# Preparation of a bidirectional layer by halves of the batch and on 128 rows, with gate projections of 32 rows each

## The reference, cut to what matters

```
xn     = layernorm over channels of X
for direction in (forward, backward, on the flipped sequence):
    z, xbc, dt = split(xn @ in_proj)                 # z: 64 gates, xbc: 64 x + 16 B + 16 C, dt: 4 heads
    x, B, C    = split(silu(depthwise_conv4(xbc)))   # causal, 4 taps
    dt         = softplus(dt + dt_bias);  a = -exp(A_log) * dt
    y          = sum over earlier tokens of (C.B) * exp(sum of a between them) * x * dt,  + D * x
    out       += rmsnorm(y * silu(z)) @ out_proj
X = X + average of both directions
```

## Time and profile before

| | |
|---|---|
| median of 3 runs (lowest, highest) | 698.82 us (697.15, 700.01) |
| the profiled execution: its time, span from first to last instruction | 702.39 us, 700.5 us |
| busy: PE, DVE, ACT, share of the span | 71%, 44%, 46% |
| mean granted TensorE clock | 0.740 of 2.4 GHz |

### The profile page before, as it was taken

The page is one execution under the profiler, slowest core; times in us unless marked ns, Lnnn a source line. Parts: engine busy times, 40 slices in busy tenths (PEclk is TensorE's granted clock), DMA queues, the critical chain, the costliest instruction groups (busy, mean ns, idle before and its releaser), DMA issues.

```text
span 700.5 us, 10770 instructions
## 1 busy us (share of the span) xinstructions
PE 495.4 (71%) x3956; PEld 274.8 (39%) x3957; DVE 308.5 (44%) x724; ACT 320.1 (46%) x1085; POOL 0.2 (0%) x4
## 2 busy tenths in 40 slices
PE   5654555556987689999855666666576898989633
PEld 2221222223663567677513333333322454455211
DVE  1174000006883678888751000000018896477443
ACT  2232333333672767777633333333335655655411
POOL 0000000000000000000000000000000000000000
PEclk9555555556899899999985555555568999999877
DMA  4000000000000000000000000000024110000000
GB/s 190 0 2 1 0 1 1 0 1 0 2 1 1 0 2 1 1 2 1 1 0 1 0 1 1 0 1 0 1 43 98 39 36 1 1 2 3 0 9 32
DMA packets 9389, 8.37 MB, mean 12 GB/s; under 512 B 3314, under 2 KB 9074, under 8 KB 9204
## 3 DMA queue, kind: packets, MB, share of 16 engines
q1 hardware_dynamic: 9332, 7.62, 3.8%
HBM read 4.99 MB, written 0.52 MB: 8 GB/s over the span
## 4 chain that ended last, share of the span: by engine, by line
PE 58%; DVE 16%; ACT 15%; issue 7%; SPq 1%; DMA 1%; DVEq 1%; ACTq 0%
PE ps L317 16%; ACT arena L335 10%; PE ps L295 4%; PE ps L300 3%; PE ps L620 2%; PE ps L637 2%; PE ps L817 2%; PE ps L781 2%; PE ps L624 2%; DVE arena L1316 2%; PE ps L651 2%; DVE arena L1325 2%; PE ps L796 2%; PE ps L257 2%; PE ps L785 2%
## 5 line engine op out<-in xcount | busy, mean ns | idle before, releaser
L317 PE MATMUL ps<-arena,wsb 16*16 16x16 f32 (+1 forms) x1024 | 131.5, 206 | 116.9 <-ACT arena L335 111.4
L335 ACT ACTIVATE arena<-ps 16x16 f32<-16x16 f32 (+1 forms) x512 | 96.0, 188 | 192.4 <-PE ps L317 192.4
L317 PEld LDWEIGHTS ps<-arena,wsb 16*16 16x16 f32 (+1 forms) x1024 | 76.7, 118 | 200.3 <-ACT arena L335 186.9
L341 DVE TENSOR_TENSOR X<-X,ps 128x128 f32<-128x128 f32 x16 | 4.6, 287 | 199.6 <-PE ps L300 199.5
L1033 ACT ACTIVATE arena<-ps,arena 128x128 f32<-128x128 f32 (+1 forms) x128 | 52.3, 418 | 31.1 <-DVE arena L1317 31.0
L1121 ACT ACTIVATE arena<-ps 128x512 f32<-128x512 f32 x72 | 40.9, 595 | 25.9 <-PE ps L785 20.4
L1467 DVE TENSOR_TENSOR arena<-arena,ps 128x512 f32<-128x512 f32 x64 | 41.8, 682 | 16.0 <-ACT arena L1121 13.6
L1316 DVE TENSOR_REDUCE arena<-ps 128x2 f32<-128x512 f32 (+1 forms) x48 | 33.0, 688 | 18.3 <-PE ps L620 10.9
L637 PE MATMUL ps<-wsb,arena 128*128 128x128 f32 x192 | 30.7, 283 | 11.3 <-DVE arena L1325 11.2
L624 PE MATMUL ps<-arena 128*128 128x256 f32 x128 | 35.4, 400 | 0.0
L1325 DVE TENSOR_TENSOR arena<-arena 128x512 f32<-128x512 f32 x48 | 33.3, 693 | 1.7
(11 more groups left out here) (267 smaller groups left out, 764.5 us busy)
## 6 DMA issues: line engine op xcount, KB each, us to landing
wsb<-weights SPq DMA_DIRECT2D x1, 2060.5 KB, 9.2
arena<-xn SPq DMA_DIRECT2D x16, 128.0 KB, 2.5
arena<-w SPq DMA_DIRECT2D x20, 64.0 KB
wsb<-weights SPq DMA_DIRECT2D x1, 549.5 KB, 4.3
X<-x SPq DMA_DIRECT2D x1, 512.0 KB, 3.4
out<-arena SPq DMA_DIRECT2D x2, 256.0 KB, 2.3
arena<-w_biases SPq DMA_DIRECT2D x20, 17.0 KB
csb<-consts SPq DMA_DIRECT2D x1, 128.0 KB, 9.1
```

The costliest lines, as they stand in the source:

```text
L317: nc.tensor.matmul(step_columns(k, rows, r), w_state, states[0:rows, :, :, t].rearrange("p g j -> p (g j)"), start=False, stop=True, skip_ ...
L335: nc.scalar.activation(states[0:rows, :, :, t + 1].rearrange("p g j -> p (g j)"), step_columns(t // STEP_BANK, rows, t % STEP_BANK), func) ...
```

## The change

The stack is made in two sets of 16 DMAs, first columns of j = 0, 1 for all taps and groups, as soon as half 0 of `xn` is there, then j = 2, 3. The first direction's x, B and C are projected and passed through silu half by half, in banks given by `FIRST_X` and `FIRST_BC`. dt lies on 128 rows by 512 columns (half h in rows 64h to 64h + 63) in place of 64 by 1024; scans are four, the three bf16 parts are made for both directions at once on 128 rows in `sum_parts`, and `place_sums` copies the rows of one direction into `c3`, six copies. Two of the eight operands of the first direction are made in slot 1 of its loop. The first direction's exponents use bank (n + 2) % 4, its first C.B products come after exponent 1, and only exponent 2 waits for `xdt`. `project_z` issues eight matmuls of 32 rows by 64 columns per direction, one for each batch group and half, each reading only its group's partitions. The diff at its core:

```diff
+FIRST_X, FIRST_BC = ((5, 6), (0, 1)), ((7, 2), (4, 3))
+TURNED = ((5, 6, 0, 1), (0, 1, 2, 3))
...
-        def decay_part(link, d, part):
-
-            rows, dst = cs[ROWS * d:ROWS * (d + 1)], c3[ROWS * part:ROWS * (part + 1)]
-            link(nc.vector.tensor_copy(dst, rows))
-            if part < 2:
-                link(nc.vector.tensor_tensor(rows, rows, dst, ALU.subtract))
+        def place_sums(d):
+
+            for part in range(3):
+                for h in range(2):
+                    ins = nc.vector.tensor_copy(c3[ROWS * part:ROWS * (part + 1), 2 * h:2 * h + 2],
+                                                sum_parts[E2 * h + ROWS * d:E2 * h + ROWS * (d + 1), part])
+            return ins
...
-            sp.wait_ge(s["normalised"], 8)
-            for i in range(K):
-                for g in range(G):
-                    sp.dma_start(xs[C * i:C * i + C, :, g, K - 1 - i:K - 1 - i + T],
-                                 xn[C * g:C * g + C, :].rearrange("p (j t) -> p j t", j=J)).then_inc(s["M stack"], 16)
+            sp.wait_ge(s["normalised"], 7)
+            for h in range(2):
+                if h == 1:
+                    sp.wait_ge(s["normalised"], 8)
+                for i in range(K):
+                    for g in range(G):
+                        sp.dma_start(xs[C * i:C * i + C, 2 * h:2 * h + 2, g, K - 1 - i:K - 1 - i + T],
+                                     xnj[C * g:C * g + C, 2 * h:2 * h + 2, :]).then_inc(s[("M stack", "M stack rest")[h]], 16)
...
-                mm = nc.tensor.matmul(ps[0:2 * ROWS, 4 + h, :], W("M_dtW"), halves(xn)[h], start=True, stop=True)
+                pe.wait_ge(s["normalised"], 7 + h)
+                mm = nc.tensor.matmul(ps[E2 * h:E2 * (h + 1), 4, :], W("M_dtW"), halves(xn)[h], start=True, stop=True)
...
-                for gp in range(2):
-                    for h in range(2):
-                        nc.tensor.matmul(ps[:, 2 * gp + h, :], W(("fwd", "bwd")[d] + "_z")[:, gp * P:(gp + 1) * P], halves(xn)[h],
-                                         start=True, stop=True).then_inc(s["M z proj"], 1)
+                for h in range(2):
+                    for g in range(G):
+                        rows, gp, gl = slice(C * g, C * (g + 1)), g // 2, g % 2
+                        mm = nc.tensor.matmul(ps[E2 * gl:E2 * (gl + 1), 2 * gp + h, :],
+                                              W(("fwd", "bwd")[d] + "_z")[rows, gp * P + gl * E2:gp * P + (gl + 1) * E2],
+                                              halves(xn)[h][rows, :], start=True, stop=True)
+                        if gl == 1:
+                            mm.then_inc(s["M z proj"], 1)
...
             project_z(0)
             pe.wait_ge(s["M weights"], 1)
             pe.wait_ge(s["M stack"], 16 * K * G)
+            project_x_first(0)
+            pe.wait_ge(s["M dt"], 1)
...
+            mm.then_inc(s["M dt turned"], 1)
+            project_bc_first(0, 0)
+            pe.wait_ge(s["M stack rest"], 16 * K * G)
             pe.wait_ge(s["M z"], 4)
-            project_x(0)
...
+            project_x_first(1)
+            pe.wait_ge(s["M dt by token"], 1)
+            project_bc_first(1, 0)
+            project_bc_first(0, 1)
+            project_bc_first(1, 1)
...
+                    if d == 0 and n == 2:
+                        pe.wait_ge(s["M xdt"], 1)
+                    if d == 0 and n == 5:
+                        pe.wait_ge(s["M decay operands"], 2)
...
-                    gp, h = k // 2, k % 2
+                    gp, h = k % 2, k // 2
                     act.wait_ge(s["M z proj"], 4 * d + k + 1)
...
             for part in range(3):
-                decay_part(link, 0, part)
-            for k in range(G + HEADS):
+                link(nc.vector.tensor_copy(sum_parts[:, part], cs))
+                if part < 2:
+                    link(nc.vector.tensor_tensor(cs, cs, sum_parts[:, part], ALU.subtract))
+            link(place_sums(0))
+            for k in (0, 1, 4, 5, 6, 7):
                 ins = decay_operand(0, k)
...
                         if d == 0:
+                            for k in (2, 3):
+                                ins = decay_operand(0, k)
+                            ins.then_inc(s["M decay operands"], 1)
...
-                    if d == 0 and n in (8, 10, 12):
-                        decay_part(link, 1, n // 2 - 4)
+                    if d == 0 and n == 8:
+                        dve.wait_ge(s["M decay operands"], 2)
+                        link(place_sums(1))
```

More of the change, by code:

```diff
@@ L746, in _ @@
                 for i in range(2):
[L747 to L750, removed]
+                    if d == 0:
+                        continue
+                    pe.wait_ge(s["M mean squares saved"] if i == 0 else s["M out saved"], 2 if i == 0 else 1)
                     for h in range(2):
@@ L758, in _ @@
                     project_z(1)
-                pe.wait_ge(s["M decay operands"], d + 1)
-                pe.wait_ge(s["M xdt"], d + 1)
-                pe.wait_ge(s["M C"], d + 1)
+                pe.wait_ge(s["M decay operands"], 1 if d == 0 else 3)
+                if d == 1:
+                    pe.wait_ge(s["M xdt"], 2)
+                pe.wait_ge(s["M C"], d + 2)
                 pe.wait_ge(s["M z"], 4 * (d + 1))
@@ L784, in exponent, with cb_products @@
                     c0 = j * T + block_of(d, which) * P
-                    nc.tensor.matmul(ps[:, n % 4, :], key_side[d][g // 2][:, g % 2, c0:c0 + P],
+                    nc.tensor.matmul(ps[:, ring(n), :], key_side[d][g // 2][:, g % 2, c0:c0 + P],
                                      query_side[d][:, :, c0:c0 + P], start=False, stop=True).then_inc(s["M exponent"], 1)
[L787 to L799, removed]
+                def cb_products(k):
+                    if k < 8:
+                        pe.wait_ge(s["M B split"], G * d + (2 if k == 0 else 4))
+                    if k >= 8:
+                        pe.wait_ge(s["M gram"], ALL * d + slot_of(k - 5) + 1)
+                    for i in range(4):
+                        one, piece = near_unit(k + i)
+                        at0 = block_of(d, piece) * P
+                        mm = nc.tensor.matmul(ps[:, 4 + k // 4 % 2, i * P:(i + 1) * P],
+                                              bz[:, one % G, one // G, at0:at0 + P],
+                                              cpj[:, one // G, at0:at0 + P], start=(i == 0), stop=(i == 3))
+                    mm.then_inc(s["M CB"], 1)
                 def near_products(k):
@@ L1088, in squares, with silu_x_first @@
                 nc.scalar.activation(zf[:, j, :], yg[:, j, :], ACT.Square).then_inc(s["M squares"], 1)
+            def silu_x_first(h):
+                for gp in range(2):
+                    act.wait_ge(s["M x proj"], 2 * h + gp + 1)
+                    nc.scalar.activation(xf[:, 2 * h:2 * h + 2, gp * T:(gp + 1) * T],
+                                         ps[:, FIRST_X[h][gp], :].rearrange("p (j t) -> p j t", j=2), ACT.Silu, bias=W("fwd_bx"))\
+                        .then_inc(s["M x"], 1)
@@ L1090, in _, with silu_bc_first @@
+            def silu_bc_first(i, h, n):
+                act.wait_ge(s["M bc"], n)
+                nc.scalar.activation(halves((bp, cp)[i])[h], ps[:, FIRST_BC[i][h], :], ACT.Silu, bias=W(("fwd_bB", "fwd_bC")[i]))\
+                    .then_inc(s[("M B", "M C")[i]], 1)
             gates(0)
             for d in range(2):
-                name = ("fwd", "bwd")[d]
-                if d == 1:
-                    act.wait_ge(s["M y"], J)
[L1096 to L1099, removed]
-                                         ps[:, k, :].rearrange("p (j t) -> p j t", j=2), ACT.Silu, bias=W(name + "_bx"))\
-                        .then_inc(s["M x"], 1)
@@ L1102, in _ @@
-                if d == 0:
-                    act.wait_ge(s["M dt turned"], 1)
-                    nc.scalar.activation(dtt.rearrange("p a b -> p (a b)"), ps[:, 6, :], ACT.Copy).then_inc(s["M dt by token"], 1)
-                if d == 1:
+                if d == 0:
+                    silu_x_first(0)
+                    act.wait_ge(s["M dt turned"], 1)
+                    nc.scalar.activation(dtt.rearrange("p c h r -> p (c h r)"), ps[:, 4, :], ACT.Copy).then_inc(s["M dt by token"], 1)
+                    silu_bc_first(0, 0, 1)
+                    silu_x_first(1)
+                    silu_bc_first(1, 0, 2)
+                    silu_bc_first(0, 1, 3)
+                    silu_bc_first(1, 1, 4)
+                else:
+                    act.wait_ge(s["M y"], J)
+                    for k in range(4):
+                        gp, h = k // 2, k % 2
+                        act.wait_ge(s["M x proj"], 4 * d + k + 1)
+                        nc.scalar.activation(xf[:, 2 * h:2 * h + 2, gp * T:(gp + 1) * T],
+                                             ps[:, k, :].rearrange("p (j t) -> p j t", j=2), ACT.Silu, bias=W("bwd_bx"))\
+                            .then_inc(s["M x"], 1)
@@ L1396, in _ @@
```

(1 more changed line is left out.)

102 lines of the change are left out of this document (53 added, 49 removed).

## The result

The kernel after the change takes 705.79 us, the median of 4 runs (702.8 to 707.86); the kernel before, run beside it on the same chip, 697.99 us (4 runs). The ratio is 1.0107, 95% interval 1.0056 to 1.0159. The change costs about 1.1%, some 7.5 us. The profiled execution took 706.23 us, with a span of 704.4 us and a mean granted clock of 0.739 (before: 702.39, 700.5, 0.740).

The account below looks back on a forecast made before the run. The prediction took stack transfers, then PE and DVE, to bound the first direction's preparation, and PE its loop. First product +4.9, operands +0.8, loop end -0.5 and gates -0.9 gave +4.3 on 698.82, so 703.1 us, range 695 to 706.5.

Parts of the forecast that it names:

- The issue time goes with the form: Stack DMAs on SP's queue: halving the bytes leaves the time from issue to issue at 0.63 us; chance 0.60.
- follows the bytes: Rival for the stack issues: spacing falls to 0.34 us with the bytes, giving 692.5 us; chance 0.15.
- the two-row stores: Rival for the stack issues: each takes 0.49 us, as two-row stores to memory did, giving 698.0 us; chance 0.17.
- T2: First direction's preparation: moment the stack's second half is usable, forecast at 540.9 us, 8.0 us after the stack before.
- The chain behind T2: First direction: work left from T2 to the loop's first product, 10.5 us at full clock.
- The clock, "I take 1.6 (0 to 2.4)": Work behind T2: PE's lower clock level after idling some 4 us adds 1.6 us, range 0 to 2.4.
- Two operands in slot 1: First direction's loop: two operands moved into slot 1 stand between products on DVE, counted as +0.8 us.
- The loop's pace: Loop slots 9 to 32: PE sets the pace, so they stay unchanged at 24.6 us.
- The end of the loop: First direction, slot 32 to last product: six small copies replace `decay_part`, -0.5 us (0 to -0.6).
- Gates: Second direction's gate projections: 32-row matmuls run together in fours and ACT sets the end, -0.9 us (0 to -1.0).
- Serial gate matmuls: Rival for the gate projections: matmuls run one after another, 6.9 us in place of 3.7, giving 707.2 us; chance 0.05.
- The preparation on 128 rows is covered: First direction's dt and operands on DVE: the saving on 128 rows is hidden by the late stack, DVE needed only about 547.

Follow-up runs that it names:

- e3: Kernel before, each of the 16 stack DMAs moving one 1 KB row in place of four (output not the reference's): 697.1 us, single run.
- e2: Kernel before with the stack made by 32 DMAs in two halves, PE waiting for all of them at once: 706.29 us, ratio 1.0115.
- e6: Changed kernel plus six useless matmuls keeping PE busy ahead of its wait for the stack's second half: 701.94 us, ratio 1.0068 to the kernel before.
- e5: Kernel before with only the gate projections changed, to eight matmuls of 32 rows per direction, and the gates in that order: 696.14 us, ratio 0.997.
- e1: Changed kernel with the stack made again by 16 DMAs of both halves: 697.12 us, ratio 0.9986 to the kernel before.
- e4: Changed kernel with the last 12 of the 32 stack DMAs issued by ACT, the others by SP: 698.05 us, ratio 1.0001 to the kernel before.
- e8: Changed kernel, each half's stack 10 issues on SP and 6 on ACT, x turned by halves before B and C, eight operands before the loop: 692.45 us.
- e7: Changed kernel with 16 stack DMAs, x turned before the last three quarters of B and C, all eight operands before the loop: 698.59 us, ratio 0.9995.

## Why the prediction came out as it did

It forecast 703.1 us and slower; it is 705.79 and slower, inside the range and 2.7 above the forecast, but above the 701 to 705.5 that the forecast's own terms gave. As a difference, +4.3 us was forecast and some +7.5 measured. The first product, forecast at 552 to 554, came at 555.7 on the count of the kernel before (518.14 + 37.57). The mechanism held, and one term was too small.

- **The issue time goes with the form: right.** 32 issues, 0.66 us apart (21.15 / 32), for half the bytes; e3 shows it for a quarter. The rivals "follows the bytes" (0.34) and "the two-row stores" (0.49) fall with it. By the Trainium skill (Perfetto Trace Analysis, DMA Optimizations) splitting may let some transfers start sooner where the DMA engines are generally idle; here the queue, not the engines, was full, and e2 shows that the split alone costs 1.15%.
- **T2, 540.9 forecast: nearly right.** Counted from `xn` it was forecast 22.76 us behind (540.9 - 518.14) and came 23.42 behind: 0.66 more. The last issue started 20.55 us after the first, not 19.5, half of it because one of them took 1.11 us; the way from it to the work was 2.1 us, not 2.5.
- **The chain behind T2, at full clock 10.5 us: right.** e6 took 10.73.
- **The clock, "I take 1.6 (0 to 2.4)": this is the term that was mis-sized.** The kernel after takes 14.15 us behind T2, so it was 3.65, beyond its upper end too; PE had waited 5.79 us, not some 4. x took 3.61 from T2 to B and C where 1.7 were counted, B and C 3.75 where 2.7, the C.B products with their handover 1.91 where 1.2, and the turning, `times_dt` and `split_b` what was forecast. I took two thirds of the 2.4 us that one x projection had lost. Here all of the second half's x and the start of B and C had the lower level, and a second stretch followed at the C.B products, which the forecast did not know. With e6's extra matmuls both are gone. Had this term been 3.65, the forecast would have been 705.2 us. First product: 0.66 + 2.05 of clock make 2.7 on top of +4.9, and it was +7.58.
- **Two operands in slot 1, +0.8: right**, +0.93 (9.21 us from the first product to slot 9 against 8.28). **The loop's pace: right**, 24.59 us from slot 9 to 32. **The end of the loop, -0.5: right**; slot 32 to the last product took 6.29 against 6.71, so -0.4. **Gates, -0.9: right**, -1.14, here and in e5.
- **Serial gate matmuls: wrong**, as expected. 16 matmuls of 0.43 us would take 6.9 and took 1.95. The Trainium skill (TensorEngine Tiling (Array Packing), Restrictions and Gotchas) has different row tiles unable to access one PSUM bank at the same time; on separate partitions of a bank this case does not bear that out.
- **The preparation on 128 rows is covered: right**, DVE idles 15.31 us behind it.

With the measured terms the sum is 7.58 + 0.93 - 0.42 - 1.14 = +6.95 us; the timed ratio gives 7.5, with an interval of 3.9 to 11.1. That the table has +6.88 at the next norm is in part luck: 1.6 us that the forecast did not know were gained ahead of the second direction, 1.3 of them by the clock, and 1.6 were lost again behind it (+5.32 there, +6.88 at the norm). e1 and e2 close the account from both sides: without the split no loss, with the split alone all of it.

## What to carry to other kernels

Before a transfer is split so that work may start on its first part, ask what paces the issues: look at the engine's queue beside the DMA share, and if the issues follow each other without a gap, expect a split to lengthen them: here 16 issues of 10.52 us became 32 of 21.15, with the DMA engines at 0.44. Try a second queue for the issues first. And price PE's waits twice: once for the wait and once for the work behind it, which may run at half the clock. That can happen at a later and shorter wait of the chain too; here the same wait of 2.05 us had it in one kernel and not in three others.

## What the runs showed of the hardware

- A DMA of 32 partitions within SBUF takes the issuing queue 0.63 to 0.69 us from one to the next (16 in 10.15 and 10.52 us, 32 in 20.65 to 21.97), with 128, 64 or 32 KB in it. ACT's queue has the same pace (12 in 7.89 us, 11 in 7.10), and both run at it side by side. The Trainium skill (DMA: Bandwidth & Descriptors, Issuing engines are not separate DMA queues) says that starting DMAs on several engines saves only the sequencer's time, which is usually small next to the DMA; here an issue is 0.60 of the 0.66 us from one DMA to the next, and e4 (ratio to the kernel before 1.0001, with one queue 1.0107) and e8 gained from it.
- The granted clock fell to 1.2 GHz behind waits of PE of 5.79 and, in the kernel after, of 2.05 us, and cost 3.4 us in a chain of 14. In e6 the same wait of 2.05 us, with PE kept busy in the earlier one, left the clock at 2.4 GHz, as it did in e1 and e4. A wait of 1.44 us left it there in e1 (x projection 3.65 us) and not in e7 (5.35 us).
- Sixteen matmuls of 32 rows by 64 columns by 512 run four at a time, 1.95 us for all, with two row groups writing one bank.
